# Layer norm, transposes and first key products by turns, the first weights ahead of x, and an edge table put in a row by TensorE

## The reference

```python
xn = _layernorm(x, axis=-1)
x = x + _L0_gnn_ref(xn, edge_index, edge_type_3, ...) + _L0_mix_ref(xn[None], W_qkv, b_qkv, W_out, b_out)[0]
x = x + _L0_ffn_ref(_layernorm(x, axis=-1)[None], weight_t, bias)[0]

# _L0_mix_ref: linear attention, 12 heads of 64
qkv = x @ W_qkv + b_qkv
qf, kf = _phi(q), _phi(k)            # where(x > 0, x + 1, exp(x))
kv = einsum("bhnd,bhne->bhde", kf, v)
y = (qf @ kv) / max(qf @ kf.sum(n), EPS)
return y @ W_out + b_out

# _L0_gnn_ref: two attention convolutions over the edges, softmax by target node
```

## Time and profile before

| | us |
|---|---|
| median of 3 runs | 1630.11 (1629.23 to 1632.68) |
| the profiled execution's own time | 1625.55 |
| its span, first to last instruction | 1623.5 |
| PE busy in it | 1542.9 (95%) |
| DVE busy | 1255.2 (77%) |
| ACT busy | 816.8 (50%) |
| POOL busy | 206.7 (13%) |

### The profile page before, as it was taken

How to read it: one execution, slowest core, us unless ns; L and a number is a source line. 1 busy time by engine, 2 the same in 40 slices (tenths; PEclk the granted TensorE clock), 3 DMA queues, 4 the chain that set the end, 5 groups by cost and what they waited for, 6 DMA issues and landing times.

```text
span 1623.5 us, 34809 instructions
## 1 busy us (share of the span) xinstructions
PE 1542.9 (95%) x10294; PEld 1100.0 (68%) x10295; DVE 1255.2 (77%) x2652; ACT 816.8 (50%) x1079; POOL 206.7 (13%) x473
## 2 busy tenths in 40 slices
PE   5799999999999999999999999979999999999987
PEld 3355556776566666899999999965556555555544
DVE  7388878995699993788998989854772677777795
ACT  6233324652445652788888888752222333333352
POOL 4013212310000000000000000000000243343340
PEclk9899999999999999999999999979999999999998
DMA  6113113624576645500042312045665701101302
GB/s 195 30 67 112 47 63 113 222 89 120 181 218 197 197 140 174 171 32 32 32 119 74 105 56 80 16 123 152 200 193 180 252 1 57 58 0 58 105 25 95
DMA packets 127719, 177.74 MB, mean 109 GB/s; under 512 B 15981, under 2 KB 99158, under 8 KB 127629
## 3 DMA queue, kind: packets, MB, share of 16 engines
q1 hardware_dynamic: 127628, 176.62, 34.7%
HBM read 119.69 MB, written 56.89 MB: 109 GB/s over the span
## 4 chain that ended last, share of the span: by engine, by line
PE 71%; issue 16%; DVE 7%; DMA 2%; ACT 1%; DVEq 1%; POOL 1%; POOLq 0%; SPq 0%; ACTq 0%
PE ps L2261 23%; PE ps L2215 15%; PE ps L2320 8%; PE ps L2321 8%; PE ps L2039 3%; PE ps L2022 2%; PE ps L2023 2%; PE ps L2024 2%; DVE oh_q L1544 1%; PE ps L2332 1%; DVE oh_p L1545 1%; PE ps L2198 1%; PE ps L2076 1%; DMA tab_d<-tab 1%; DMA fx<-y_d 1%
## 5 line engine op out<-in xcount | busy, mean ns | idle before, releaser
L2261 PE MATMUL ps<-xrh,pf 128*128 (+1 forms) x2400 | 399.0, 329 | 4.8 <-DVE pf L1796 4.8
L2261 PEld LDWEIGHTS ps<-xrh,pf 128*128 128x128 f32 x2400 | 392.5, 190 | 11.2 <-issue 8.8
L2320 PE MATMUL ps<-x,ph 128*128 (+1 forms) x600 | 196.4, 327 | 12.0 <-POOL pl L1041 11.9
L2022 PE MATMUL ps<-w_hi,xt_hi 128*128 128x384 f16 x600 | 197.8, 330 | 3.2 <-DVE ev L1842 3.2
L1796 DVE SCALAR_TENSOR_TENSOR pf<-vb,CT 128x1260 f32<-128x1260 f32 x118 | 172.9, 1468 | 33.7 <-PE ps L2261 33.7
L2321 PE MATMUL ps<-x,ph 128*128 (+1 forms) x600 | 197.8, 330 | 0.0
L2023 PE MATMUL ps<-w_lo,xt_hi 128*128 128x384 f16 x600 | 197.4, 329 | 0.0
L2024 PE MATMUL ps<-w_hi,xt_lo 128*128 128x384 f16 x600 | 197.1, 328 | 0.0
L1544 DVE TENSOR_SCALAR oh_q<-pat,cw 125x420 f16<-125x420 uint16 x450 | 146.3, 325 | 44.9 <-PE ps L2039 33.1
L1792 DVE SCALAR_TENSOR_TENSOR vb<-vb,tb 128x1260 f32<-128x1260 f32 x118 | 170.0, 1467 | 12.9 <-ACT vb L1292 12.1
L1704 DVE CUSTOM_DVE_ANT_0 tt_junk<-kbc,mb 126x1260 bf16<-126x1260 f32 x120 | 169.1, 1466 | 10.6 <-issue 10.6
(11 more groups left out here) (279 smaller groups left out, 2472.0 us busy)
## 6 DMA issues: line engine op xcount, KB each, us to landing
qbc<-tq_d SPq DMA_DIRECT2D x12, 1260.0 KB, 6.5
wst<-in_L_gnn_W SPq DMA_DIRECT2D x60, 192.0 KB, 2.9
xr_d<-ev SPq DMA_DIRECT2D x60, 192.0 KB, 2.1
x_d<-ev SPq DMA_DIRECT2D x60, 192.0 KB, 2.3
mb_d<-mb SPq DMA_DIRECT2D x30, 310.1 KB
mb<-mb_d SPq DMA_DIRECT2D x30, 310.1 KB
xrh<-xr_d SPq DMA_DIRECT2D x3, 2880.0 KB, 15.5
x<-x_d SPq DMA_DIRECT2D x2, 3840.0 KB, 19.9
```

Source lines behind the costliest of these rows:

```text
L2022: pe.matmul(ps[:, bank, 0:CW], a_hi, hi[:, k, :], start=(k == 0 and not bias), stop=False)
L2261: mm = pe.matmul(out[b], pf[j][:, b * DB:b * DB + P], x, start=(first and b % 2 == 0), stop=False, skip_group_check=True)
L2320: pe.matmul(ps[:, bank, 0:CW], p, cols(off, off + CW), start=start, stop=False, skip_group_check=True)
```

## The change

It has four parts.

1. In SP's list the bias and chunk 0 of the weights are read ahead of x. POOL splits the bias before it begins with the layer norm, and the round trip of the bias through DRAM (kb_d, krow) is issued right behind x, ahead of the edges.
2. The transposes of a pair of blocks use banks 0 to 3 only, so products in banks 4 to 7 can stand between them. The lists of PE, ACT and DVE take turns: transposes of pair 0, product 0, transposes of pair 1, products 1 and 2, and so on. DVE's list has the key steps, statistics, low parts and tables in a new order; ACT's has w_hi of chunk 0 first.
3. The row of window words is made by PE: one matmul of the column of first tiles with the identity, one of the column of groups with the triangle of ones, both onto one partition of PSUM; DVE copies them into tabrow. The stores to tab_d and the load from it are gone.
4. POOL, DVE, ACT and PE wait for e_row (DVE's copies) where they waited for tab_io (the load).

The core of the diff:

```diff
 # SP
+            sp.dma_start(kbias[:, :], bqkv[D:3 * D].rearrange("(p c) -> p c", c=2 * K6)).then_inc(ob_io, 16)
+            sp.dma_start(wst[0][:, :, :], CH[0]).then_inc(w_in[0], 16)
             for p in range(NB // 2 - 1):
                 sp.dma_start(X[:, 2 * p:2 * p + 2, :], ...).then_inc(x_in[p], 16)
...
+            sp.wait_ge(ob_step, 5)
+            sp.dma_start(kb_d.rearrange("j (p c) -> p j c", c=2 * K6), ksplit[:, :, :]).then_inc(ob_io, 16)
+            sp.wait_ge(ob_io, 32)
+            sp.dma_start(krow[:, :], kb_d[:, :]).then_inc(ob_io, 16)
...
-            sp.wait_ge(e_row, 7)
-            sp.dma_start(tab_d[0:1, 0:NTAB].rearrange("o w -> w o"), tab16[:, 0:1]).then_inc(tab_io, 16)
-            sp.dma_start(tab_d[0:1, NTAB:2 * NTAB].rearrange("o (w c) -> w (o c)", c=2), tab16[0:NTAB // 2, 1:3]).then_inc(tab_io, 16)
-            sp.wait_ge(tab_io, 32)
-            sp.dma_start(tabrow[:, :].bitcast(U16), tab_d[:, :]).then_inc(tab_io, 16)
 # DVE, the end of tables
-                    dve.tensor_copy(tab16[:, 0:1], tab[:, 0:1])
-                    dve.tensor_copy(tab16[0:NTAB // 2, 1:3], ps[0:NTAB // 2, 0, 0:2]).then_inc(e_row, 1)
+                    dve.tensor_copy(tabrow[:, 0:NTAB // 2].bitcast(U16), ps[0:1, 0, 0:NTAB])
+                    dve.tensor_copy(tabrow[:, NTAB // 2:NTAB].bitcast(U16).rearrange("o (w c) -> o w c", c=2),
+                                    ps[0:1, 0, NTAB:2 * NTAB].rearrange("o (c w) -> o w c", c=2)).then_inc(e_row, 1)
 # PE, table_sums
+                pe.wait_ge(tl_done, 2 * NB + 4)
+                pe.matmul(ps[0:1, 0, 0:NTAB], tab[:, 0:1], ident[0:NTAB, 0:NTAB], start=True, stop=False, skip_group_check=True)
+                pe.matmul(ps[0:1, 0, NTAB:2 * NTAB], tab[:, 1:2], ltri[:, :, :].rearrange("p c w -> p (c w)"), start=False, stop=True, skip_group_check=True).then_inc(e_tr, 1)
 # PE, the order
+            def first_product(i):
+
+                pe.wait_ge(tl_done, 2 * i + 6)
+                if i >= 4:
+                    pe.wait_ge(kv_out, i - 1)
+                product(0, xt_hi, xt_lo, i, 4 + i % 4, True).then_inc(g_done, 1)
+            pair_transposes(0)
             pe.wait_ge(w_lo_done, 1)
-            pe.wait_ge(ob_io, 32)
...
+            pe.wait_ge(ob_io, 48)
+            first_product(0)
+            pair_transposes(1)
+            first_product(1)
+            first_product(2)
+            pair_transposes(2)
+            first_product(3)
+            first_product(4)
+            pair_transposes(3)
+            first_product(5)
+            pe.wait_ge(tl_done, 2 * 8 + 4)
+            table_rows()
+            first_product(6)
+            pe.wait_ge(e_row, 1)
+            pair_transposes(4)
+            first_product(7)
+            table_sums()
+            first_product(8)
+            first_product(9)
+            pe.wait_ge(e_row, 7)
 # DVE, the order
+            pair_stats(0)
             w_lo_part(0)
+            pair_stats(1)
+            pair_low(0)
+            pair_stats(2)
+            pair_low(1)
+            first_key(0)
+            pair_stats(3)
+            first_key(1)
             tables(0)
+            first_key(2)
+            pair_stats(4)
+            pair_low(2)
             tables(1)
+            w_lo_part(1)
+            first_key(3)
+            first_key(4)
+            pair_low(3)
+            first_key(5)
+            tables(2)
+            tables(3)
+            first_key(6)
+            tables(4)
+            pair_low(4)
+            tables(5)
+            first_key(7)
+            dve.wait_ge(e_row, 7)
+            dve.wait_ge(pat_done, 1)
+            count_part(0)
+            for n in range(8, NB):
+                first_key(n)
 # ACT, the order
+            w_hi_part(0)
+            normalise(0)
+            high_parts(0)
+            normalise(1)
+            first_keys(0)
+            high_parts(1)
...
```

More of the change, by code:

```diff
@@ L1069, in w_hi_part, with normalise, high_parts @@
                 act.activation(w_hi[c % 2][:, :, :], wst[c % 2][:, :, :], ACT.Copy).then_inc(w_hi_done, 1)
-            for p in range(NB // 2):
-                for j in range(2):
-                    n = 2 * p + j
+            def normalise(p):
+                for n in (2 * p, 2 * p + 1):
                     act.wait_ge(nmr_done, 2 * n + 2)
-                    act.activation(xn[j][:, :], X[:, n, :], ACT.Identity, bias=nmr[:, n % 4, :], scale=rstd[:, n % 4, :]).then_inc(ln_done, 1)
+                    act.activation(xn[n % 2][:, :], X[:, n, :], ACT.Identity, bias=nmr[:, n % 4, :], scale=rstd[:, n % 4, :]).then_inc(ln_done, 1)
+            def high_parts(p):
                 for j in range(2):
@@ L1098, in keys, with first_keys @@
                 act.activation(ev_m[j][:, :], ev_m[j][:, :], ACT.Exp, scale=-1.0).then_inc(kv_e, 1)
-            for n in range(NB):
+            def first_keys(n):
                 act.wait_ge(g_done, n + 1)
@@ L1104, in _ @@
                 keys(n, 4 + n % 4, n % 4)
+            w_hi_part(0)
[4 more added lines that the diff above has]
+            high_parts(1)
+            normalise(2)
+            first_keys(1)
+            w_hi_part(1)
+            first_keys(2)
+            high_parts(2)
+            normalise(3)
+            first_keys(3)
+            first_keys(4)
+            high_parts(3)
+            normalise(4)
+            first_keys(5)
+            first_keys(6)
+            high_parts(4)
+            for n in range(7, NB):
+                first_keys(n)
             w_hi_part(2)
@@ L1521, in pair_low, with pair_stats @@
                         lo_half(2 * p + j, j, hf)
-            for p in range(NB // 2):
+            def pair_stats(p):
                 dve.wait_ge(x_in[p], 16 if p < NB // 2 - 1 else 32)
@@ L1999, in table_sums, with pair_transposes @@
                 pe.wait_ge(e_const, 2)
-                for c in range(2):
-                    last = pe.matmul(ps[0:NTAB // 2, 0, c:c + 1], ltri[:, c, :], tab[:, 1:2], start=(c == 0), stop=(c == 1), skip_group_check=True)
-                last.then_inc(e_tr, 1)
-            for p in range(NB // 2):
+                pe.wait_ge(tl_done, 2 * NB + 4)
+                pe.matmul(ps[0:1, 0, 0:NTAB], tab[:, 0:1], ident[0:NTAB, 0:NTAB], start=True, stop=False, skip_group_check=True)
+                pe.matmul(ps[0:1, 0, NTAB:2 * NTAB], tab[:, 1:2], ltri[:, :, :].rearrange("p c w -> p (c w)"), start=False, stop=True, skip_group_check=True).then_inc(e_tr, 1)
+            def pair_transposes(p):
                 for j in range(2):
@@ L2008, in _ @@
                     for hf in range(2):
-                        if p >= 2:
-                            pe.wait_ge(tl_done, 2 * i + hf + 1 - 4)
+                        if p >= 1:
+                            pe.wait_ge(tl_done, 2 * i + hf + 1)
                         for k in range(3):
-                            last = pe.transpose(ps[:, 4 * (p % 2) + 2 * j + hf, k * P:(k + 1) * P], xn[j][:, (3 * hf + k) * P:(3 * hf + k + 1) * P], ident[:, :])
+                            last = pe.transpose(ps[:, 2 * j + hf, k * P:(k + 1) * P], xn[j][:, (3 * hf + k) * P:(3 * hf + k + 1) * P], ident[:, :])
                         last.then_inc(tr_done, 1)
```

55 lines of the change are left out of this document (10 added, 45 removed).

## The result

The changed kernel takes 1617.79 us (median of 4 runs, 1616.76 to 1619.28). The kernel before took 1631.39 us beside it (median of 4, 1629.23 to 1633.16). The ratio is 0.9922 [0.9904, 0.994], which is 12.7 us; the medians themselves are 13.6 us apart. The profiled execution took 1616.76 us with a span of 1614.7 us, which is 8.8 us less than the profiled one of before.

A forecast was written before the change was run, and what follows sets the result against it. PE is busy 95% of the span, so only its stalls and slow stretches ahead of 81 us yield time. Product 10 ending at 72.1 instead of 81.0, less 0.4 us, saves 8.5: 1630.1 to 1621.6 us, range 1615.5 to 1627.0.

The forecast's parts named there:

- Product 0's start: First key product on PE, waiting for the bias row krow: starts at about 20.6 us, bounds 18.8 and 23.3.
- Its clock: Product 0 after a pause of PE: partly at half clock, 2.2 us lost, bounds 0 and 2.9, end at 26.1 us.
- Products 1 to 7 between the transposes: PE's products and transposes taking turns: 31.6 us of work plus waits of 1.0 and 0.7 us, end at 59.4 us.
- The word: Edge word made by PE without DRAM: ready at 60.3 us, first one-hots from 64.2, product 10 can start at 68.8 us.
- Product 10's clock: Product 10 after a wait of 2.4 us: full clock holds, so 3.3 us instead of 6.0, end at 72.1 us.
- The sum: End of product 10: 81.0 less 72.1 is 8.9 us, less 0.4 for handovers between engines, 8.5 us saved.
- The words on the ten products: The first ten products end no sooner, 66.4 against 65.3 us, because transposes now lie among them.
- the median of three runs lies 4.6 us above it: Whole kernel: from 1617.0 us for the profiled execution to a median of 1621.6 us, 1630.1 less 8.5.
- A: Bias row ahead of product 0: krow lands at 25 to 29 us, saving only 0 to 4 us; chance 0.16.
- D: Ahead of product 10: it waits as long for something else, such as late one-hots, 1630 us; chance 0.02.
- B: Product 0: krow at 18.8 us or full clock, saving 11 to 13 us, 1618 us; chance 0.13.
- C: Products among the transposes: clock stays at half, 2.7 us per product, up to 1646 us; chance 0.05.

The follow-up runs named there:

- second trace of before: The kernel before with no edit, profiled a second time: median 1631.3 us, ratio to itself 1.0018, span 1628.2 us.
- the second comparison: The changed kernel with no edit, timed again beside the kernel before and profiled a second time: median 1619.1 us, ratio 0.9932.
- the run with the bias last: Changed kernel with key step 8 ahead of the first one-hots and the bias row's matmul last in the first ten products: 1614.0 us, ratio 0.9905.

## Why the prediction was right

The time fell inside the range; 1621.6 us was predicted and 1617.8 us measured, 0.2 us below the band of 1618 to 1626 us that was held likeliest. Step by step, predicted and then as traced:

- *Product 0's start*: 20.6, traced 20.25 us. Two errors cancel: kb_d landed at 17.75 us (17.0 taken), krow took 2.40 us (3.53 taken).
- *Its clock*: 2.2 us, traced 1.9. The product ended at 25.42 instead of 26.1 us.
- *Products 1 to 7 between the transposes*: 33.3 with waits of 1.7, traced 32.7 us with waits of 2.56 (1.65 and 0.91). The groups of transposes were priced at 1.79 us and took 1.40.
- *The word*: ready 0.9 us after table_sums, predicted and traced. To the first one-hot 3.76 us (3.93 predicted). PE's wait 2.23 us (2.4 predicted).
- *Product 10's clock*: "the clock should hold" was wrong. It fell to 0.50 within product 10 after a pause of only 2.2 us, and cost 1.6 us. I had read it from one hole, where it fell 5 us after PE's last work. In the second trace of before PE's last work ended at 67.2 us and the clock fell between 69 and 70 us, less than 3 us later:

```profile
69.00:70.00 1.00, 0.00 (x0) 0.00 (x0) 0.00 (x0) 1.00 (x1) 0.00 (x0) 0.70 1.05 396
```

  Product 10 began 1.4 us sooner than predicted, which hid the miss by luck: its end was predicted for 72.1 us, traced 72.3.
- *The sum*: 8.5 us. Counts of 81.05 and 72.34 us give 8.7, the spans 8.8. Its parts differ more than the sum: the wait brought 7.4 us (7.3 predicted), product 10's clock 1.1 (2.7), and product 9 ended 0.2 us sooner (1.1 later predicted). That the shift stays the same to the end is luck of this pair; in the second pair it is 11.2 us at the counts and 8.4 us in the spans.
- *The words on the ten products*, "no sooner than before (66.4 against 65.3 us)": this rested on one trace of before, the earliest. In five traces of the old order without the early reads product 9 ended at 65.3, 66.0, 67.2, 67.6 and 68.7 us, 67.0 on the mean; in the four of the changed order with krow's trip at 65.3, 64.8, 65.2 and 65.9. By these means, 67.0 and 65.3, the turns carry some 1.7 us there, in spite of the 3.7 us that the early reads alone cost at the counts; with so few traces this is an estimate.

The term that missed is the last one: "the median of three runs lies 4.6 us above it". I subtracted the saving of one trace from the median, as if before's profiled run and its saving belonged to each other. The first trace of before was 4.7 us shorter than its second, while the changed kernel's first lay 1.0 us under its median. With two traces of each, the counts moved by 9.9 us on the mean (82.1 to 72.2), while four pairs of spans give anything from 3.7 to 13.5 us. The medians give 13.6 us and, in the second comparison, 9.7 us; the ratios 12.7 and 11.1 us. So the gain is about 10 to 13 us. About 10 of it is traced to the stage ahead of the counts; where the rest comes from, and how much of it is chance, these runs don't settle.

The rivals: A is out (krow landed at 20.16 us), D too. B, krow at 18.8 us or product 0 at full clock, did not happen, though its 1618 us was nearer the time; what it says of DVE ("becomes the limit soon") is refuted by the run with the bias last. C is out: the spacing stays at 0.16 us through four groups of transposes and two waits. The rule weighed beside it (the Trainium skill, TensorE: Matmul & The Clock Gate, Part 4: PE-mode transpose) has the trace against it once more. In the second trace of before PE did nothing but transposes for 31 us, and the clock rose in the pause right behind a group (0.50, 0.80 and 1.00 in the rows; product 0's matmuls behind it are 0.16 us apart):

```profile
30.50:31.40 0.90, 0.87 (x5) 0.47 (x3) 0.81 (x3) 0.61 (x2) 0.00 (x0) 0.50 0.10 12
31.40:32.50 1.10, 0.00 (x0) 0.00 (x0) 1.02 (x3) 1.09 (x2) 0.00 (x0) 0.80 0.78 182
32.50:33.50 1.00, 0.96 (x6) 0.53 (x7) 0.97 (x3) 1.00 (x1) 0.00 (x0) 1.00 1.03 373
```

## What to carry to other kernels

Look first at what is queued behind a late datum, and only then at the datum: one key step moved ahead of the one-hots took 7 us off PE's wait while the DRAM trip stayed, though product 10 still ran at half clock. A long trip through DRAM that only turns a column into a row costs less as a matmul onto one partition, 0.9 us in place of 17. The row that arrives last (the bias) can stand at the end of its sum instead of at its start; here that brought product 9 forward by 2.7 us. And before a difference of a few us is read from two traces, profile the same program twice: here one program differed from itself by 5 us in its span, partly in short stretches where the clock fell or held behind the same wait, and by 2.9 us in its median.

## What was not expected of the hardware

- Behind a pause of PE of 2.2 us, with full work on both sides, the clock fell within product 10 in all three traces that have it (at 68.82 us in the first trace of the changed kernel). Behind pauses of 2.57 us it had held in seven traces and fallen in seven, and both happened with the same program.
- The edge words' store of 2-byte elements over 96 partitions took 13.4 to 13.8 us in all five traces that have it; it hardly varies.
- A POOL operation on one column took 2.48 us in place of 0.19 beside a DVE operation of 2.52 us with two inputs from SBUF. It moved with that operation, and ended with it. By the Trainium skill (SBUF — State Buffer, SBUF: two separate sides) the second read port of DVE and that of GpSimd are one, and whoever comes second is blocked for the whole instruction; the traces agree.
